# Attention with V as the held operand: high parts of the odd key chunks by a second exponential on ScalarE, of the even ones by a GpSimd cast

## What is computed

```python
inp = layernorm_c(x) + 2.0 * sinu
q = conv2d(inp, wq)                       # 1x1, 256 channels
k, v = conv2d(inp, wk, 1, 1), conv2d(inp, wv, 1, 1)   # 3x3, 256 channels each
q, k = rotary(split_heads(q)), rotary(split_heads(k)) # 8 heads of 32
attn = softmax(einsum('bhid,bhjd->bhij', q, k) * SCALE)
attn = einsum('bhij,hg->bgij', attn, mix)             # the heads are mixed
out = einsum('bhij,bhjd->bhid', attn, v)
o = conv2d(out.reshape(B, 256, H, W), wo) + bo
a, g = split(o, 2, axis=1)
x = x + a * sigmoid(g)
t = to_tokens(x)
t = t + ffn(layernorm(t))       # router, top 2 of 8 experts, 128 -> 512 -> 128
```

## Time and profile before

| | us |
|---|---|
| runs | 3077.63, 3080.15, 3084.39 |
| median | 3080.15 |
| profiled execution | 3081.93 |
| its span | 3080.2 |
| TensorE busy | 2951.5 (96%) |
| VectorE busy | 2193.4 (71%) |
| ScalarE busy | 1446.3 (47%) |
| GpSimd busy | 1331.2 (43%) |
| mean granted clock of TensorE | 0.986 of full |

### The profile page before, as it was taken

The page is one execution under the profiler, slowest core; times in us unless marked ns, Lnnn a source line. Parts: engine busy times, 40 slices in busy tenths (PEclk is TensorE's granted clock), DMA queues, the critical chain, the costliest instruction groups (busy, mean ns, idle before and its releaser), DMA issues.

```text
span 3080.2 us, 54552 instructions
## 1 busy us (share of the span) xinstructions
PE 2951.5 (96%) x20354; PEld 2717.5 (88%) x20354; DVE 2193.4 (71%) x3332; ACT 1446.3 (47%) x1862; POOL 1331.2 (43%) x996
## 2 busy tenths in 40 slices
PE   8999999999999999999999999999999999948996
PEld 6999889998999899988999899979998899837776
DVE  4677768775877587776877687758776787655663
ACT  2455335542555255534554355525552455436671
POOL 3244424542454334542454245433454246227783
PEclk9999999999999999999999999999999999969998
DMA  3364010101110101101010111010110111127665
GB/s 116 132 230 153 5 41 22 44 10 35 30 30 25 36 22 23 40 16 32 22 46 9 35 32 30 23 36 22 25 39 19 28 32 52 50 92 264 232 223 206
DMA packets 71429, 196.94 MB, mean 64 GB/s; under 512 B 16136, under 2 KB 16722, under 8 KB 71158
## 3 DMA queue, kind: packets, MB, share of 16 engines
q1 hardware_dynamic: 62070, 176.40, 18.7%
q0 software_dynamic: 9088, 16.94, 1.7%
HBM read 40.43 MB, written 63.34 MB: 34 GB/s over the span
## 4 chain that ended last, share of the span: by engine, by line
PE 89%; issue 4%; ACT 3%; DMA 2%; DVE 2%; POOL 1%; SPq 0%; POOLq 0%; ACTq 0%; DVEq 0%
PE PV L629 49%; PE ST L629 25%; PE MX L629 13%; DMA wt<-wall 1%; ACT h L1003 1%; ACT xr L1003 1%; DMA wall<-yrows 0%; ACT E L1003 0%; PE PV L759 0%; PE PV L717 0%; DVE El L1304 0%; POOL yrows L597 0%; PE MX L932 0%; PE PV L948 0%; DVE mcol L1299 0%
## 5 line engine op out<-in xcount | busy, mean ns | idle before, releaser
L515 POOL TENSOR_TENSOR acc<-acc,tmp 128x256 f32<-128x256 f32 x512 | 802.3, 1567 | 1372.2 <-DVE tmp L1314 1372.2
L629 PE MATMUL PV<-vh,El 128*128 128x258 f32 x4096 | 1185.2, 289 | 11.9 <-DVE vl L1294 7.9
L629 PE MATMUL PV<-vh,Eh 128*128 128x258 f32 x4096 | 1154.5, 282 | 0.0
L629 PE MATMUL PV<-vl,Eh 128*128 128x256 f32 x4096 | 1149.9, 281 | 0.0
L1003 ACT ACTIVATE Eh<-ST 128x1024 fp32r<-128x1024 f32 x512 | 524.9, 1025 | 765.4 <-PE ST L629 765.4
L1299 DVE TENSOR_REDUCE mcol<-MX 128x1 fp32r<-128x1024 f32 x512 | 625.8, 1222 | 348.7 <-PE MX L629 346.5
L629 PEld LDWEIGHTS PV<-vh,El 128*128 128x128 f32 x4096 | 772.5, 189 | 43.3 <-DVE El L1304 8.8
L629 PEld LDWEIGHTS PV<-vl,Eh 128*128 128x128 f32 x4096 | 778.0, 190 | 24.5 <-issue 3.8
L629 PEld LDWEIGHTS PV<-vh,Eh 128*128 128x128 f32 x4096 | 772.6, 189 | 0.0
L1304 DVE TENSOR_TENSOR El<-E,Eh 128x1024 fp32r<-128x1024 f32 x512 | 632.2, 1235 | 9.9 <-ACT E L1003 9.8
L1003 ACT ACTIVATE E<-ST 128x1024 f32<-128x1024 f32 x512 | 521.6, 1019 | 0.0
(11 more groups left out here) (219 smaller groups left out, 3154.1 us busy)
## 6 DMA issues: line engine op xcount, KB each, us to landing
rows<-xr SPq DMA_DIRECT2D x68, 520.0 KB, 5.7
kst<-src SPq DMA_DIRECT2D x192, 128.0 KB
...
```

The source lines that it names most:

```text
L515: nc.gpsimd.tensor_tensor(acc[:, ic, :], acc[:, ic, :], tmp[:, p, :], ALU.add).then_inc(s_acc, 1)
L629: return nc.tensor.matmul(o, w, m, start=start, stop=stop)
```

## The change

A unit is now one head and 512 queries (16 units a batch), and the operands of `values` are exchanged.

- **values**: a 128x128 block of V (keys by channels, vh or vl) is held, and 512 columns of Eh or El move: for each chunk, two halves c of the channels and three products, 48 matmuls of 512 columns a unit. The output has channels on its partitions, as the output projection wants it: `out_transpose` is gone, and `out_hi` splits a half of acc (128x1024) by one copy.
- **scores**: per chunk one matmul of 512 columns, into ST0 and ST1 in turn, one bank each.
- **The sum of a row** no longer comes out of `values`. ScalarE's `sums` takes the exponential of `max_scores`' output in place (128x1024, bias the negative maximum, accumulating the sum), VectorE's `shifts` works out -(max + log sum) from it in 14 operations on 128x4 numbers, and `max_row` (four matmuls, with the identity moving) and `row_copy` put it into two rows of `qst`, a high and a low part. So E comes out normalised, and `normalise` is gone.
- **max_scores** run against the banks MA and MB in turn, four for a unit; in the convolution stage all but the last of them use MA alone.
- **exps**: per chunk of 512 columns ScalarE makes E32 (a ring of four); for odd chunks Eh too, by a second exponential. For even chunks GpSimd's `cast` makes Eh from E32. `exp_lo` is 512 wide, eight a unit, and waits for the cast on even chunks.
- **evict**: ScalarE copies the two halves of PV, scaled by mix (one number per channel), to tmp, or in units 0 and 1 of a batch straight to acc; GpSimd adds tmp to acc, 2 x (128x512) a unit.
- **The order in the convolution stage**: the two output projections stand directly after pieces 3 and 5, the first maxima in the middle of piece 7 (before: after piece 9). On VectorE the gate of the first half stands ahead of `rotate(4)`, and before it stood behind `rotate(5)`.
- Batch 7 is written out too, so the loop is over six.

```diff
-def scores(n, k, p):
-    st, q, _ = par_of(k)
-    if p == 0:
-        wait(pe, s_mrow, n + 1)
-    wait(pe, s_ex, 2 * n + p - 1)
-    for j in range(4):
-        jc = 4 * p + j
-        last = mm(ST[p][:, j * QT:(j + 1) * QT], kst[st][:, jc * P:(jc + 1) * P],
-                  qst[st][:, q * QT:(q + 1) * QT], True, True)
-    last.then_inc(s_st, 1)
+def scores(b, u, kc):
+    n, (par, cols) = b * UNITS + u, heads_of(u)
+    if kc == 0:
+        pe.wait_ge(s_mrow, n + 1)
+    wait(pe, s_ex, KC * n + kc - 1)
+    mm(ST[kc % 2][:, :], kst[par][:, kc * P:(kc + 1) * P], qst[par][:, cols], True, True).then_inc(s_st, 1)
...
-def values(n, k, p, jcs):
-    e = k % 2
-    for jc in jcs:
-        if jc == 0:
-            wait(pe, s_nrm, 2 * n + p + 1)
-        if p == 0 and jc % 4 == 0:
-            wait(pe, s_lo, 2 * n + jc // 4 + 1)
-        hi, lo = (t[:, e, jc, p * P:(p + 1) * P] for t in (Eh, El))
-        mm(PV[p][:, 0:VW], lo, vh[:, jc, :], jc == 0, False)
-        mm(PV[p][:, 0:INNER], hi, vl[:, jc, :], False, False)
-        last = mm(PV[p][:, 0:VW], hi, vh[:, jc, :], False, jc == KC - 1)
-    if KC - 1 in jcs:
+def values(b, u, kc):
+    n = b * UNITS + u
+    pe.wait_ge(s_lo, KC * n + kc + 1)
+    for c in range(2):
+        if u == 0 and kc == 0:
+            wait(pe, s_vlo, b * 4 + 3 + c)
+        if kc == 0:
+            wait(pe, s_ev, 2 * n - 1 + c)
+        cols = slice(c * P, (c + 1) * P)
+        last = split3(PV[c], vh[:, kc, cols], vl[:, kc, cols], Eh[:, kc, :], El[:, kc, :], kc == 0, kc == KC - 1)
+        if kc == KC - 1:
+            last.then_inc(s_o, 1)
+    if kc < KC - 1:
         last.then_inc(s_pv, 1)
...
-def max_scores(n, k, p, head=None):
-    st, q, _ = par_of(k)
-    if p == 0:
-        wait(pe, s_mrow, n)
-        if q == 0:
-            wait(pe, s_stk[st], head)
-    else:
-        wait(pe, s_red, 2 * n + 1)
-    for i in range(2):
-        last = mm(MX[:, i * NB:(i + 1) * NB], qst[st][0:MROW, q * QT + p * P:q * QT + (p + 1) * P],
-                  kst[st][0:MROW, i * NB:(i + 1) * NB], True, True)
+def max_scores(b, u, i, M, free):
+    n, (par, _) = b * UNITS + u, heads_of(u)
+    if i == 0 and u % 2 == 0:
+        wait(pe, s_stk[par], b * 384 + (u // 4 + 1) * 96)
+    wait(pe, s_l, free)
+    q = u % 2 * NB + i * P
+    for j in range(2):
+        last = mm(M[:, j * NB:(j + 1) * NB], qst[par][0:MROW, q:q + P],
+                  kst[par][0:MROW, j * NB:(j + 1) * NB], True, True)
     last.then_inc(s_mx, 1)
...
-def max_row(n, k):
-    wait(pe, s_red, 2 * n + 2)
-    for p in range(2):
-        last = mm(MX[:, p * P:(p + 1) * P], mcol[:, k % 2, p, :], negid[:, :], True, True)
+def max_row(b, u, free):
+    n = b * UNITS + u
+    wait(pe, s_ch, NCH * n + NCH)
+    wait(pe, s_l, free)
+    for i in range(QC):
+        last = mm(MA[0:2, i * P:(i + 1) * P], mc[:, u % 2, i, :], identr[:, :], True, True)
     last.then_inc(s_mt, 1)
...
-def exps(n, k, p):
-    wait(act, s_st, 2 * n + p + 1)
-    copy(Eh[:, k % 2, 4 * p:4 * p + 4, :].rearrange("p a b -> p (a b)"), ST[p][:, :], ACT.Exp, scale=SCALE)
-    wait(act, s_lo, 2 * n + p - 1)
-    copy(E32[:, p, :], ST[p][:, :], ACT.Exp, scale=SCALE).then_inc(s_ex, 1)
+def exps(b, u, kc):
+    n = b * UNITS + u
+    wait(act, s_lo, KC * n + kc - 3)
+    act.wait_ge(s_st, KC * n + kc + 1)
+    if kc % 2 == 1:
+        copy(Eh[:, kc, :], ST[1][:, :], ACT.Exp)
+    copy(E32[:, kc % 4, :], ST[kc % 2][:, :], ACT.Exp).then_inc(s_ex, 1)
...
+def sums(b, u, i, M):
+    n, par = b * UNITS + u, u % 2
+    act.wait_ge(s_red, 4 * n + i + 1)
+    wait(act, s_ch, NCH * n - 2 * NCH + 2)
+    copy(M[:, :], M[:, :], ACT.Exp, bias=nmax[:, par, i:i + 1], accum_out=rsum[:, par, i:i + 1]).then_inc(s_l, 1)
...
+def evict(b, u, c):
+    n, h = b * UNITS + u, u // 2
+    act.wait_ge(s_o, 2 * n + c + 1)
+    if u >= 2:
+        wait(act, s_acc, b * ADDS + 2 * u - 5 + c if u >= 3 else b * ADDS)
+        copy(tmp[:, c, :], PV[c], scale=mix_col[:, c, h:h + 1]).then_inc(s_ev, 1)
+    else:
+        wait(act, s_olo, b * 4)
+        copy(acc[:, c, u % 2 * NB:(u % 2 + 1) * NB], PV[c], scale=mix_col[:, c, h:h + 1]).then_inc(s_ev, 1)
...
 def out_hi(n, hf):
-    for c in range(2):
-        wait(act, s_tr, n * 4 + 2 * hf + c + 1)
-        if hf == 1:
-            wait(act, s_wo, n * 2 + 1)
-        copy(oh[:, c, :], PV[c][:, :]).then_inc(s_ohi, 1)
+    wait(act, s_acc, ADDS * (n + 1))
+    copy(oh[hf], acc[:, :, hf * NB:(hf + 1) * NB]).then_inc(s_ohi, 1)
...
-def normalise(n, k, p, head):
-    wait(dve, s_pv, 2 * n + p + 1)
-    nc.vector.reciprocal(rl[:, p:p + 1], PV[p][:, INNER:INNER + 1]).then_inc(s_rl, 1)
-    m = mix_sb[:, bass.ds(head * HEADS, HEADS)].rearrange("p (g a) -> p g a", a=1).to_broadcast([P, HEADS, DH])
-    wait(dve, s_rl, 2 * n + p + 1)
-    wait(dve, s_acc, 2 * n + p + 1)
-    stt(tmp[:, p, :].rearrange("p (g d) -> p g d", d=DH), PV[p][:, 0:INNER].rearrange("p (g d) -> p g d", d=DH),
-        rl[:, p:p + 1], m, ALU.mult, ALU.mult).then_inc(s_nrm, 1)
...
-def take_max(n, k, p):
-    wait(dve, s_mx, 2 * n + p + 1)
-    nc.vector.tensor_reduce(mcol[:, k % 2, p, MROW:MROW + 1], MX[:, :], AX, ALU.max).then_inc(s_red, 1)
+def take_max(b, u, i, M):
+    n, par = b * UNITS + u, u % 2
+    dve.wait_ge(s_mx, 4 * n + i + 1)
+    nc.vector.tensor_reduce(nmax[:, par, i:i + 1], M[:, :], AX, ALU.max, negate=True).then_inc(s_red, 1)
...
+def shifts(b, u, part):
+    n, par = b * UNITS + u, u % 2
+    base, m, y, q, z = NCH * n, lman[:, par, :], lexp[:, par, :], lfit[:, par, :], shft[:, par, :]
+    bits = rsum[:, par, :].bitcast(i32)
+    if part == 0:
+        dve.wait_ge(s_l, 4 * n + 4)
...
+    if part == 1:
...
+        tt(z, z, q, ALU.subtract).then_inc(s_ch, 1)
+    if part == 2:
+        wait(dve, s_mt, n - 1)
+        dve.wait_ge(s_ch, base + 12)
+        nc.vector.tensor_copy(mc[:, par, :, 0], z).then_inc(s_ch, 1)
+        dve.wait_ge(s_ch, base + 13)
+        tt(mc[:, par, :, 1], z, f(mc[:, par, :, 0]), ALU.subtract).then_inc(s_ch, 1)
...
-def exp_lo(n, k, p):
-    wait(dve, s_ex, 2 * n + p + 1)
-    at = (slice(None), k % 2, slice(4 * p, 4 * p + 4), slice(None))
-    tt(El[at].rearrange("p a b -> p (a b)"), E32[:, p, :], f(Eh[at]).rearrange("p a b -> p (a b)"),
-       ALU.subtract).then_inc(s_lo, 1)
+def exp_lo(b, u, kc):
+    n = b * UNITS + u
+    if kc % 2 == 0:
+        dve.wait_ge(s_eh, KC // 2 * n + kc // 2 + 1)
+    else:
+        dve.wait_ge(s_ex, KC * n + kc + 1)
+    tt(El[:, kc, :], E32[:, kc % 4, :], f(Eh[:, kc, :]), ALU.subtract).then_inc(s_lo, 1)
...
-def out_transpose(n, hf):
-    if hf == 0:
-        wait(pe, s_acc, (n + 1) * 2 * UNITS + 2)
-    for c in range(2):
-        if hf == 1:
-            wait(pe, s_olo, n * 4 + c + 1)
-        for j in range(4):
-            last = nc.tensor.transpose(PV[c][:, j * P:(j + 1) * P],
-                                       acc[:, 4 * hf + j, c * P:(c + 1) * P], ident[:, :])
-        last.then_inc(s_tr, 1)
...
+def cast(b, u, kc):
+    if isinstance(b, int):
+        pool.wait_ge(s_ex, KC * (b * UNITS + u) + kc + 1)
+    else:
+        pool.wait_ge(s_ex, ready[kc // 2 % 2])
+        pool.reg_add(ready[1 - kc // 2 % 2], ready[kc // 2 % 2], 2)
+    nc.gpsimd.tensor_copy(Eh[:, kc, :], E32[:, kc % 4, :]).then_inc(s_eh, 1)
...
-def add(n, k, p):
-    ic = k % QC * 2 + p
-    wait(pool, s_nrm, 2 * n + p + 3)
-    wait(pool, s_acc, 2 * n + p + 2)
-    nc.gpsimd.tensor_tensor(acc[:, ic, :], acc[:, ic, :], tmp[:, p, :], ALU.add).then_inc(s_acc, 1)
+def add(b, u, c):
+    n = b * UNITS + u
+    cols = slice(u % 2 * NB, (u % 2 + 1) * NB)
+    wait(pool, s_acc, b * ADDS + 2 * u - 7 + c if u >= 4 else b * ADDS)
+    pool.wait_ge(s_ev, 2 * n + c + 1)
+    nc.gpsimd.tensor_tensor(acc[:, c, cols], acc[:, c, cols], tmp[:, c, :], ALU.add).then_inc(s_acc, 1)
...
 def batch(b, prev=None, more=True):
-    if prev is not None:
-        out_transpose(prev, 0)
-    conv(b, 4)
     if prev is not None:
         out_project(prev, 0)
-        out_transpose(prev, 1)
+    conv(b, 4)
     conv(b, 5)
-    conv(b, 6)
     if prev is not None:
         out_project(prev, 1)
-    conv(b, 7)
+    conv(b, 6)
+    conv(b, 7, range(0, 5))
+    max_scores(b, 0, 0, MA, 4 * n)
+    conv(b, 7, range(5, TAPS))
...
+def unit(b, u, prev, more):        
+    for kc in range(KC):
+        values(b, u, kc)
+        if u < UNITS - 1:
+            scores(b, u + 1, kc)
+        if kc == 1 and u < UNITS - 2:
+            max_scores(b, u + 2, 2, MA, 4 * n + 9)
+        if kc == 3 and u < UNITS - 2:
+            max_scores(b, u + 2, 3, MB, 4 * n + 10)
+        if kc == 5 and u < UNITS - 3:
+            max_scores(b, u + 3, 0, MA, 4 * n + 11)
+        if kc == KC - 1:
+            max_row(b, u + 2, 4 * n + 13)
+            max_scores(b, u + 3, 1, MB, 4 * n + 12)
```

More of the change, by code:

```diff
@@ L841, in batch @@
+            def batch(b, prev=None, more=True):
                 n = b * UNITS
@@ L1492, in batch @@
                 v_lo(b, 2)
+                exp_lo(b, 0, 4)
+                exp_lo(b, 0, 5)
```

(1 more changed line is left out.)

826 lines of the change are left out of this document (455 added, 371 removed).

## The result

The changed kernel takes 3307.94 us (median of 4, 3303.74 to 3310.17) against 3082.27 of the kernel before in the same comparison: ratio 1.0724, 95% interval 1.0691 to 1.0757. It is slower, as forecast, by 225 us between the two profiled executions (3306.94 against 3081.93), where the sum gave 174.

The account below looks back on a forecast made before the run. TensorE was taken to bound the kernel before, so every new wait is paid whole: 3081.93 - 45 + 122 + 97 = 3256 us profiled, 3255 for the median, range 3130 to 3385.

Parts of the forecast that it names:

- what TensorE issues: TensorE's matmuls: products and scores in 512 columns save 31 us, the dropped transposes of acc 14; together -45 us.
- new waits, convolution stage: Convolution stage: TensorE waits 16.9 us a batch, 15.8 of them new; +122 us over the kernel.
- new waits, loop: Attention loop: max_row waits 1.1 us a unit, less 26 us of earlier small waits; +97 us.
- stacks: Convolution stage: the first maxima wait 3.5 us for the first stacks' transfers, landing at 40.5 against TensorE at 37.1.
- The chain: Attention loop, one max_row to the next: scores, exponential, cast, exp_lo, shifts and reduction take 16.1 to 16.5 us against 15.3.
- x 14 units x 8 batches: Attention loop: the 1.1 us wait taken as equal in 14 units of 8 batches, 123 us.
- the slack that I had named myself: Whole kernel: VectorE (207.43 us) and ScalarE (138.16) have slack in the mean; when each result comes counts, not their sum.
- 45 us for that figure: GpSimd's cast in the loop: 769 ns in place of 0.60 us would add about 45 us, giving 3300.
- the second (the cast or the port as the pace): Rival, attention loop: a 0.9 us cast or queueing at the shared port adds 105 us, 3355; chance 0.20.
- The first: Rival: the attention loop stays covered and only the convolution stage waits; 3150 us, chance 0.17.
- the third: Rival: TensorE stays the bound, loop waits vanish and the stage waits 3 us a batch; 3035 us, chance 0.10.
- The fourth: Rival, ScalarE in the loop: accumulating a sum costs a second pass, 0.5 us more a unit; no chance of its own.

Follow-up runs that it names:

- short_gate: The changed kernel with the gate's reciprocal on 64 of 512 columns, part of the output left out; 3291.61 us, ratio to before 1.068.
- free: stage_banks with the loop reordered: shifts and the fourth maxima's reduction ahead of El, additions apart, next layer norm one chunk earlier; 2980.67 us, ratio 0.9668.
- stage_banks: The changed kernel with a new convolution-stage order and, in the loop, maxima moved behind max_row and chunks 1 to 3, shifts together at chunk 5; 3042.75 us.
- one_cast: The changed kernel with GpSimd casting chunk 0 only, ScalarE making Eh of chunks 1 to 7 by a second exponential; 3277.79 us, ratio to before 1.0634.
- short_adds: The changed kernel with GpSimd's additions into acc on 64 of 512 columns; 3280.89 us, ratio to before 1.0645.

## Why the prediction held, and where its terms were off

The sum in its own terms, for the profiled execution; measured values are start-to-start times of TensorE in the batch from 1099.7 to 1461.7, less those in the earlier trace rows's batch, times 8.

| term | forecast | measured |
|---|---|---|
| what TensorE issues | -45 | about -91 to -102 |
| new waits, convolution stage | +122 | about +125 (15.7 a batch) |
| new waits, loop | +97 | about +150 (18.9 a batch) |
| the lower clock | 0 | about +50 (6.5 a batch) |
| sum | +174 | +225 |

One batch times eight is rough. Counted the same way over the first seven batches together (whatever a start comes later than the usual step of its form is a wait, or the lower clock), TensorE issues 86 us less, the waits of the stage are 117 us more, those of the loop 122, and the lower clock costs 54: 206 us, which is what these seven batches grew by. Times 8/7 that is -98, +134, +139 and +61.

The total came within 51 us partly by luck: the forecast took 53 us too little off for what TensorE issues and put the clock's 61 at nothing, and these two all but cancel.

**The convolution stage** came out as worked out, waits 16.8 us in this batch against 16.9. TensorE's waits in the first 56 us of it, timeline of the changed kernel:

```profile
1105.96 0.50 PE L654 MATMUL PVT<-El,woh 128*128 128x512 f32 x1 [0.36 <-DVE El L1330]
...
1143.07 0.73 PE L654 MATMUL MA<-kst,qst 96*128 96x512 f32 x2 [0.66 <-DMA qst<-src]
1148.43 0.73 PE L654 MATMUL MA<-kst,qst 96*128 96x512 f32 x2 [0.83 <-ACT MA L1020]
1154.85 0.73 PE L654 MATMUL MA<-kst,qst 96*128 96x512 f32 x2 [2.00 <-ACT MA L1020]
```

First projection 0.5 (0.5 forecast), second 4.5 at 1126.56 (4), stacks 0.8 (3.5), the bank MA 3.1 (2.5), scores 1.6 (1.9), row of unit 1 5.3 (4.5). Only the stacks' term was wrong. (Its own pieces add up to an arrival at 36.6 and not 37.1, and so to a wait of 3.9.) The bytes landed at 43 us after the batch's start, later than my 40.5, but TensorE came at 42.6 and not at 37.1: it had been held up by 2.6 us of issue at the loop's start, and behind the gate's wait eleven of its matmuls ran at the lower clock; and two waits one behind the other don't add. short_gate shows the same from the other side.

**The loop.** The chain was right to 0.2 us at every link, and 1.1 a unit is what batch 0 shows in its eleven plain units. Some luck is in that too: TensorE's own 15.3 was 15.0 (max_row takes 0.24, not 0.34), and the chain's 12.15 + 0.15 to 0.35 + 4.0 is 16.3 to 16.5 and not 16.1 to 16.5, where 16.09 was measured. Both were some 0.3 too long, and the difference stayed. The step that was off is "x 14 units x 8 batches": the units are not alike. In batches 1 to 6 they take 16.2 to 18.4. The fourteen waits of the batch at 1099.7 add up to 18.1 us by their brackets, where fourteen of batch 0's 0.91 would make 12.7. The largest are those at the ends of units 4 to 7, of 2.4 and three times 1.6. There GpSimd's transfers of rows (1.0 to 1.4 us each) stand ahead of casts, and El waits for the cast:

```profile
1273.23 1.03 POOL L558 DMA_INDIRECT rows<-xr,slot  x1 [0.16 <-issue]
1274.27 0.62 POOL L527 CAST Eh<-E 128x512 fp32r<-128x512 f32 x1
1274.92 0.69 DVE L1402 TENSOR_TENSOR El<-E,Eh 128x512 fp32r<-128x512 f32 x1 [3.00 <-POOL Eh L527]
```

Side work on VectorE does it too. Timeline of VectorE in the unit that ends at 1435.63:

```profile
1429.67 0.16 DVE L1374 TENSOR_TENSOR shft<-nmax,lexp 128x4 f32<-128x4 f32 x1
1430.89 0.17 DVE L1275 TENSOR_SCALAR rs<-MB 128x8 f32<-128x8 f32 x1 [1.05 <-PE MB L654]
...
1432.90 0.17 DVE L1280 SCALAR_TENSOR_TENSOR rs<-rs 128x8 f32<-128x8 f32 x1
1433.00 0.16 DVE L1377 SCALAR_TENSOR_TENSOR lman<-lman,lfit 128x4 f32<-128x4 f32 x1
```

The reciprocal root of the next batch's layer norm, 11 small operations and 1.05 us of waiting for TensorE, lies between the first part of shifts and the second: 3.3 us in the middle of the chain. Before, these operations lay in the slack that I had named myself. TensorE has work of its own for the next batch in that unit (in free it takes 17.5 there), so of its 18.4 us the wait is only 1.4. The routing's operations stand in VectorE's queue in units 0 to 3, and the waits at the ends of units 0 and 1 are 1.4 each. "VectorE has slack in the mean" was true and of no use: a queue that has become the critical path makes every operation on it critical.

**What TensorE issues** was undersized by half. The 0.234 a matmul was measured where matmuls of 512 columns stand in another place of the program; here seven take 1.61 us, 0.230 each. Against that the three products of before, of 256 and 258 columns, run at 0.119, 0.118 and 0.125 in the mean, their scores at 0.125, and max_row at 0.085 a matmul against 0.061 with two columns held. Most of these differences are under a hundredth of a microsecond, and a batch has 2300 matmuls before and 1400 after. free, where TensorE hardly waits, lies 102 us below the kernel before, which hardly waits either, so it was worth about that. The -45 came from rounding small numbers ahead of multiplying them by large ones.

**The clock** was not in the sum. During the wait of 5 us for the row of unit 1, and in the stretches of the stage that have waits, the granted clock falls to the lower of its two levels (0.70 in the mean from 1192 to 1196 and 0.63 from 1196 to 1202, 0.52 from 1160 to 1163). Busy times of the changed kernel over 3 us of piece 8 (PEclk is the third number from the end), and two matmuls just ahead of them:

```profile
1160.00:1163.00 3.00, 3.00 (x9) 2.34 (x8) 0.00 (x0) 0.00 (x0) 0.00 (x0) 0.52 0.95 273
```
```profile
1159.10 0.63 PE L654 MATMUL ST<-xh,wch 128*128 128x512 f32 x1
1159.53 0.63 PE L654 MATMUL ST<-xl,wch 128*128 128x512 f32 x1
```

0.43 from start to start at 1.2 GHz in place of 0.24 at 2.4; 34 such in the batch, 0.19 each, 6.5 us. That every new wait is paid whole, as the prediction had it, was too little: with waits of some 35 us in the batch, the clock takes 6.5 on top. In stage_banks and free the granted clock is full through the whole of the same batch.

**The port and the cast.** The earlier trace rows held up: an El (0.68 alone) that starts 0.08 behind the start of a 1.29 us addition takes 1.77 and ends 0.56 after it. The rule of the lock in the Trainium skill ("SBUF — State Buffer", section on the two separate sides) agrees with that. The cast takes 0.61 alone, where the row had given 0.60. The figure in the Trainium skill ("GPSIMD Engine Reference", section 3.1), 0.77 us for 512 elements in the best case, is not what the cast takes. (The forecast's 45 us for that figure don't follow from its own sum either: 0.17 x 112 is 19.)

**The rivals.** one_cast and short_adds refute the second (the cast or the port as the pace) with gains of 30 and 27 us. (Its price was too high as well: 105 us takes 112 times the whole 0.93, where a growth of 0.33 at the cast and as much again makes 74.) The first and the third did not come about in this kernel. The fourth is refuted by the trace: a sum's exponential takes 1.09 and 0.20 more to read it, not a second pass. free does what the third needed, and more than its 3035, with the same operations in another order: what I had held against it, the gate's reciprocal of 3.4 us, only had to stand elsewhere, behind rotate(4), with the projections a piece later.
